# Layer-0 expert gate and up projections with their output index on partitions, from a static copy of the tile's weights

## The reference, cut to what matters

```
x = hidden_states.reshape(-1, 256)
probs = softmax(x @ w_router)
top_vals, top_idx = top_k(probs, 2)
for e in range(8):
    w_e = sum(where(top_idx == e, top_vals, 0))
    g = x @ w_gate[e] * 0.5          # 256 -> 512
    u = x @ w_up[e]                  # 256 -> 512
    h = silu(g) * u @ w_down[e] * 0.25
    out += w_e[:, None] * h
```

## Time and profile before

| what | us |
|---|---|
| median of 3 runs | 1102.59 |
| lowest, highest | 1101.93, 1104.66 |
| profiled execution, own time | 1102.88 |
| profiled execution, span | 1101.0 |
| graph attention of layer 0 | 10 to 186 |
| routing, similarity | 186 to 206 |
| mixture of layer 0, 23 tiles | 206 to 345 |
| reload, second layer's attention and mixture | 345 to 1101 |

### The profile page before, as it was taken

One profiled execution on the slowest core, in us unless ns is written; L12 is line 12 of the kernel. 1 busy time (PEld: TensorE's weight loads), 2 busy tenths in 40 slices (PEclk: granted clock), 3 DMA queues, 4 the chain that ended last, 5 costly groups with the idle time before them and its releaser, 6 DMA issues.

```text
span 1101.0 us, 20158 instructions
## 1 busy us (share of the span) xinstructions
PE 1006.5 (91%) x5934; PEld 821.6 (75%) x5934; DVE 868.8 (79%) x2642; ACT 613.7 (56%) x1748; POOL 430.9 (39%) x372
## 2 busy tenths in 40 slices
PE   4788877999996489999999999999998999999997
PEld 2455545466663368999999999999887888888886
DVE  6999996577773889878777877777868888788877
ACT  4789983533232377777787777777952222222231
POOL 5798892633321233323332333222422232233231
PEclk9968887699998699999999999999999999999999
DMA  9700003011113111010101000000011111111111
GB/s 286 257 1 2 1 2 110 27 47 49 44 39 117 60 39 49 1 39 2 49 1 40 13 23 1 2 1 1 15 30 29 44 43 52 48 43 44 56 43 38
DMA packets 49459, 49.25 MB, mean 45 GB/s; under 512 B 4896, under 2 KB 42464, under 8 KB 49376
## 3 DMA queue, kind: packets, MB, share of 16 engines
q1 hardware_dynamic: 45888, 40.83, 11.8%
q0 software_dynamic: 2208, 6.03, 1.8%
q10 hardware_dynamic: 1280, 1.38, 0.5%
HBM read 43.11 MB, written 5.11 MB: 44 GB/s over the span
## 4 chain that ended last, share of the span: by engine, by line
PE 71%; DVE 12%; ACT 7%; POOL 5%; issue 4%; DMA 1%; SPq 0%; DVEq 0%; ACTq 0%; POOLq 0%
PE bank L57 13%; PE bank L58 13%; PE bank L59 13%; PE bank L957 6%; PE bank L978 4%; PE bank L852 4%; PE bank L860 4%; PE bank L879 4%; PE bank L967 3%; PE bank L979 2%; POOL rest L1418 2%; POOL alpha L1421 1%; DVE alpha L1626 1%; ACT alpha L1069 1%; ACT alpha L1054 1%
## 5 line engine op out<-in xcount | busy, mean ns | idle before, releaser
L1483 POOL TENSOR_TENSOR rot_s<-swap,rq 128x512 f32<-128x512 f32 x64 | 88.5, 1384 | 194.7 <-ACT swap L1261 194.6
L1137 ACT ACTIVATE silu<-bank 128x512 f32<-128x512 f32 x66 | 39.4, 598 | 173.6 <-PE bank L59 173.6
L2066 DVE TENSOR_TENSOR o_ring<-bank,o_ring 128x256 fp32r<-128x256 f32 x128 | 54.2, 424 | 80.2 <-ACT o_ring L1290 78.7
L1274 ACT ACTIVATE prob<-prob,pmin 128x128 f32<-128x128 f32 (+1 forms) x256 | 113.3, 447 | 5.4 <-DVE pmin L2047 5.4
L957 PE MATMUL bank<-kv,norm 128*128 128x128 f32 (+1 forms) x512 | 106.1, 330 | 6.1 <-DVE norm L2040 5.9
L1889 DVE SCALAR_TENSOR_TENSOR xs<-bank,wt,xs 128x256 f32<-128x256 f32 x264 | 109.0, 476 | 0.1
L1439 POOL TENSOR_TENSOR gate_r<-gate_w,gate_r 128x256 fp32r<-128x256 f32 x31 | 36.4, 1175 | 177.3 <-ACT gate_r L1130 177.3
L1290 ACT ACTIVATE o_ring<-bank 128x256 fp32r<-128x256 f32 x128 | 48.3, 378 | 76.4 <-PE bank L979 76.3
L57 PE MATMUL bank<-wo_r,o_ring 128*128 128x256 f32 x256 | 82.5, 322 | 0.0
L1867 DVE TENSOR_TENSOR hidf<-silu,bank 128x512 f32<-128x512 f32 x66 | 45.4, 688 | 44.9 <-ACT silu L1137 43.2
L2059 DVE TENSOR_SCALAR prob<-prob,pinv 128x128 f32<-128x128 f32 (+1 forms) x256 | 76.9, 343 | 4.6
(11 more groups left out here) (304 smaller groups left out, 3087.0 us busy)
## 6 DMA issues: line engine op xcount, KB each, us to landing
gate_w<-in_Wg SPq DMA_DIRECT2D x33, 128.0 KB, 2.1
up_w<-in_Wu SPq DMA_DIRECT2D x33, 128.0 KB, 2.3
down_w<-in_Wd SPq DMA_DIRECT2D x33, 128.0 KB, 2.3
w_all<-in_w_gate SPq DMA_DIRECT2D x8, 512.0 KB, 10.5
w_all<-in_w_up SPq DMA_DIRECT2D x8, 512.0 KB, 10.3
w_all<-in_w_down SPq DMA_DIRECT2D x8, 512.0 KB, 10.6
wq_g<-in_Wq SPq DMA_DIRECT2D x4, 1024.0 KB, 5.8
wo_g<-in_Wo SPq DMA_DIRECT2D x4, 1024.0 KB, 5.5
```

Source lines behind the costliest of these rows:

```text
L1274: ins = act.activation(prob[:, u % 4, nt * P:nt * P + (nt + 1) * P], prob[:, u % 4, nt * P:nt * P + (nt + 1) * P], ACT.Exp, bias=pmin[:, u ...
L1483: pool.tensor_tensor(rot_s[:, m % 2].rearrange("p (b n) -> p b n", b=2), swap[:, m % 2].rearrange("p (b n) -> p b n", b=2), bcast(tab[:, 1 ...
```

## The change

Gate and up get their operands the other way round: a 128x128 block of expert weights is the stationary operand and the 128 turned token rows move, in four blocks of the inner index. The result has the inner index on partitions, which is what `down` wants. `turn_hidden` and `copy_hidden` go; VectorE's product is written to `hgT` (now a tile of its own in the place of `hid`), and waits for `y_ready` in place of `hid_turned`.

The stationary operand is read at a static address, from `tile_w`, two buffers of 2048 elements a partition that lie in `norm` and `actT`. VectorE fills both for tiles 0 and 1 at the end of the routing. For the tiles from 2 on, ScalarE copies gate and up of the tile's expert with two instructions (`copy_weights`), after the copy of the turned rows; it waits until up of two tiles before has been computed, and TensorE's gate waits for it (`w_copied`).

```diff
 def gate(j):                                                    # TensorE
     ats[j] = pe.value_load(w_at[0:1, j:j + 1], min_val=0, max_val=(E0 - 1) * WROW)
     pe.wait_ge(S["xgT_copied"], j + 1)
     if j >= 2:
         pe.wait_ge(S["gact_done"], j - 1)
-    for c in range(HC):
-        mm = pe.matmul(GB[j % 2][:], xgT[:, j % 2, c, :], flat_w[:, bass.ds(ats[j] + c * I0, I0)],
-                       start=c == 0, stop=c == HC - 1)
+    if j < 2:
+        pe.wait_ge(S["w_first"], j + 1)
+    else:
+        pe.wait_ge(S["w_copied"], j - 1)
+    for i in range(I0 // P):
+        for c in range(HC):
+            mm = pe.matmul(GB[j % 2][:, i * P:i * P + P], tile_w[j % 2][:, c * I0 + i * P:c * I0 + i * P + P],
+                           xgT[:, j % 2, c, :], start=i == 0 and c == 0, stop=i == I0 // P - 1 and c == HC - 1)
...
-def turn_hidden(j):
-    pe.wait_ge(S["hid_done"], j + 1)
-    if j >= 1:
-        pe.wait_ge(S["hgT_copied"], j)
-    else:
+def down(j):
+    pe.wait_ge(S["hid_done"], j + 1)
+    if j == 0:
         pe.wait_ge(S["sim_copied"], T)
-    for c in range(I0 // P):
-        mm = pe.transpose(HB[:, c * P:c * P + P], hid[:, j % 2, c * P:c * P + P], ident[:])
...
 for j in range(TILES + 1):
     if j < TILES:
         gate(j)
-    if j >= 1:
-        turn_hidden(j - 1)
-    if j < TILES:
         up(j)
     if j + 1 < TILES:
         turn_rows(j + 1)
...
-def copy_hidden(j):                                             # ScalarE
-    act.wait_ge(S["hid_turned"], j + 1)
-    if j >= 2:
-        act.wait_ge(S["y_ready"], j - 1)
-    act.activation(hgT[:, j % 2].rearrange("p c n -> p (c n)"), HB[:], ACT.Copy).then_inc(S["hgT_copied"], 1)
+def copy_weights(j):
+    at = act.value_load(w_at[0:1, j:j + 1], min_val=0, max_val=(E0 - 1) * WROW)
+    act.wait_ge(S["up_ready"], j - 1)
+    for m in range(2):
+        ins = act.activation(tile_w[j % 2][:, m * GU:m * GU + GU], flat_w[:, bass.ds(at + m * GU, GU)],
+                             ACT.Copy)
+    ins.then_inc(S["w_copied"], 1)
...
 for j in range(TILES + 1):
     if j < TILES:
         gates(j)
-    if j >= 1:
-        copy_hidden(j - 1)
     if j + 1 < TILES:
         copy_rows(j + 1)
+    if 2 <= j + 1 < TILES:
+        copy_weights(j + 1)
     if j >= 1:
         copy_out(j - 1)
...
+dve.wait_ge(S["w_all_in"], 16 * 3 * E0)                         # VectorE, end of router0
+dve.wait_ge(S["rows_out"], 16 * B)
+for j in range(2):
+    at = dve.value_load(w_at[0:1, j:j + 1], min_val=0, max_val=(E0 - 1) * WROW)
+    dve.tensor_copy(tile_w[j][:, 0:2 * GU], flat_w[:, bass.ds(at, 2 * GU)]).then_inc(S["w_first"], 1)
...
 if j >= 2:                                                      # VectorE, the product
-    dve.wait_ge(S["hid_turned"], j - 1)
-dve.tensor_tensor(hid[:, j % 2, :], gact[:, j % 2, :], UB[j % 2][:], ALU.mult).then_inc(S["hid_done"], 1)
+    dve.wait_ge(S["y_ready"], j - 1)
+dve.tensor_tensor(hgT[:, j % 2].rearrange("p c n -> p (c n)"), gact[:, j % 2, :], UB[j % 2][:], ALU.mult
+                  ).then_inc(S["hid_done"], 1)
```

More of the change, by code:

```diff
@@ L162, in build @@
         wa_tmp1 = flat(kv)[:, 2 * D:6 * D].rearrange("p (a n) -> p a n", a=4)
-        hgT = flat(norm)[:, 0:2 * I0].rearrange("p (a c n) -> p a c n", a=2, c=I0 // P)
+        tile_w = (flat(norm), flat(actT))
         x1T = route[:].rearrange("p a t e -> p (a t e)")[:, 0:2 * HC * N].rearrange("p (a c n) -> p a c n", a=2, c=HC)
@@ L219, in build @@
         gact = sb_sparse("gact", [P, 2, I0])
-        hid = sb_sparse("hid", [P, 2, I0])
+        hgT = sb_sparse("hgT", [P, 2, I0 // P, P])
         yg = sb_sparse("yg", [P, 3, D])
@@ L315, in build @@
             "xg_turned", "xgT_copied", "gate_ready", "up_ready", "gact_done", "hid_done",
-            "hid_turned", "hgT_copied", "y_ready", "y_copied", "tok_added", "sig_kept", "sig_scaled", "gam_half",
+            "w_first", "w_copied", "y_ready", "y_copied", "tok_added", "sig_kept", "sig_scaled", "gam_half",
             "qk_ready", "qk_copied", "sim_ready", "sim_copied", "sig_done", "gam_done",
@@ L833, in sparse_mixture @@
             def sparse_mixture():
-                GB, UB, XB, HB, YB = bank[0:2], bank[2:4], bank[4], bank[5], bank[6:8]
+                GB, UB, XB, YB = bank[0:2], bank[2:4], bank[4], bank[6:8]
                 flat_w = w_all[:].rearrange("p e m n -> p (e m n)")
@@ L858, in up @@
                         pe.wait_ge(S["hid_done"], j - 1)
-                    for c in range(HC):
-                        mm = pe.matmul(UB[j % 2][:], xgT[:, j % 2, c, :], flat_w[:, bass.ds(ats[j] + (GU + c * I0), I0)],
-                                       start=c == 0, stop=c == HC - 1)
+                    for i in range(I0 // P):
+                        for c in range(HC):
+                            mm = pe.matmul(UB[j % 2][:, i * P:i * P + P],
+                                           tile_w[j % 2][:, GU + c * I0 + i * P:GU + c * I0 + i * P + P],
+                                           xgT[:, j % 2, c, :], start=i == 0 and c == 0, stop=i == I0 // P - 1 and c == HC - 1)
                     mm.then_inc(S["up_ready"], 1)
-                def turn_hidden(j):
+                def down(j):
                     pe.wait_ge(S["hid_done"], j + 1)
-                    if j >= 1:
-                        pe.wait_ge(S["hgT_copied"], j)
-                    else:
+                    if j == 0:
                         pe.wait_ge(S["sim_copied"], T)
-                    for c in range(I0 // P):
-                        mm = pe.transpose(HB[:, c * P:c * P + P], hid[:, j % 2, c * P:c * P + P], ident[:])
-                    mm.then_inc(S["hid_turned"], 1)
-                def down(j):
-                    pe.wait_ge(S["hgT_copied"], j + 1)
                     if j >= 2:
@@ L1180, in sparse_mixture @@
             def sparse_mixture():
-                GB, XB, HB, YB = bank[0:2], bank[4], bank[5], bank[6:8]
+                GB, XB, YB = bank[0:2], bank[4], bank[6:8]
+                flat_w = w_all[:].rearrange("p e m n -> p (e m n)")
                 def copy_rows(j):
@@ L1794, in router0 @@
                     chain.link(dve.tensor_reduce(w_tok[:, k, :], pick[:], X, ALU.add))
+                flat_w = w_all[:].rearrange("p e m n -> p (e m n)")
+                dve.wait_ge(S["w_all_in"], 16 * 3 * E0)
[3 more added lines that the diff above has]
+                    dve.tensor_copy(tile_w[j][:, 0:2 * GU], flat_w[:, bass.ds(at, 2 * GU)]).then_inc(S["w_first"], 1)
             def router1(half, part):
```

## The result

The changed kernel takes 1123.71 us (median of 4 runs, 1122.96 to 1124.80); the kernel before took 1103.62 in the same comparison. The ratio is 1.0181, with a 95% interval of 1.0167 to 1.0195: slower, by 20.1 us. The forecast was 1123.5. The profiled execution has a span of 1123.0 us, 22.0 more than before.

The account below looks back on a forecast made before the run. TensorE alone bound the mixture at 5.83 us a tile; with the change a loop through ScalarE's copies would. +22.4 us in the loop and -1.5 at the end gave +20.9, 1123.5 us, range 1111 to 1134.

Parts of the forecast that it names:

- Gate and up at 1.78: Layer 0 mixture, TensorE: gate and up cost 1.78 us each instead of 1.72, +0.12 us a tile.
- rival C: Gate and up on TensorE: weight loads lie bare, 3.0 us each, 1178 us in all; chance 0.03.
- Turning goes: Mixture, TensorE: the hidden values' four transposes, 0.44 us a tile, leave the chain; -1.5 us from gate 22 on.
- The copies: ScalarE, from tile 2 on: two weight copies of 128x1024 a tile, 1.04 us each, 1.98 together.
- The register load: ScalarE, behind the row copy's wait: the first weight copy starts 0.70 us after the row copy starts.
- The loop: Mixture, gate to gate through ScalarE's copies: 6.90 us a tile, 144.9 against 122.49 us, +22.4.
- The first two tiles: VectorE after the last w_tok: two 128x2048 weight copies of 2.56 us each, costing the total 0.
- Rival B: Mixture stage: the clock falls as TensorE stands 16% of the time, 21 periods take 168 us, 1147 us; chance 0.10.
- Rival D: Between row copy and gate: weight copies keep ahead of TensorE, 5.51 us a tile, 1094 us; chance 0.06.

Follow-up runs that it names:

- the first experiment: Against the changed kernel, ScalarE copies the next tile's weights before the next tile's rows; 1096.25 us, ratio 0.9929 to the kernel before.

## Why the prediction was right

*Gate and up at 1.78.* Measured 1.79 for up and, after a wait, 2.02 for the gate, against 1.78 and 2.04. The value projection in the earlier trace rows was the right row: the shape and the fresh blocks were the same. The rule of the Trainium skill weighed there ("TensorE: Matmul & The Clock Gate", section "Back-to-back issue gap") would have had an estimated 0.8 us more a tile; the measured price of the operand order is 2.5 to 3.8 us in all, so for these fp32 matmuls the measurement stands against it, and against rival C.

*Turning goes.* The forecast had 0.44 us a tile, and a net 1.5 at the end. The end came out at 7.28 us from gate 22 to the end of the last down, the sum to the hundredth, and the kernel before without the turning shows 12.1 us for the whole of it.

*The copies.* Mean 1.05 us each and 2.01 for two, against 1.04 and 1.98. The Trainium skill, in "ScalarE: Activation LUTs", section "What ACT_TABLE_LOAD costs", has 186 ns + 0.833 ns an element and an overlap of about 93 ns; an estimate from it is 1.04 and 1.99, and the trace agrees.

*The register load.* 0.64 us from row copy to first weight copy against 0.70. Moving the load alone gave 0.36 us a tile. On VectorE the same load was put too low: from the last w_tok's end (203.80) to the first copy (204.85) it is 1.05 us and not 0.6, without consequence here.

*The loop.* 6.86 us a tile (215.17 to 359.31 for 21 tiles) against 6.90: 144.1 in place of 144.9. Its place in the queue is shown from two sides: the copies moved, or left out, give the same 1096; half of them taken out of the gate's wait gives back 20.4 us of an expected 20.

*The first two tiles.* VectorE's copies took 1.33 and 1.21 us, half of my 2.56; the first gate waited for the row copy and not for them.

*Rival B* did not come about: the clock in the stage stayed at 1.00. Its price was also summed wrongly. By its own terms, 4.04 us doubled for 38% of the time add 1.5 us a tile, so the 21 periods take 177 us and not 168, and the kernel some 1156 and not 1147.

*Rival D* is what the first experiment turns the kernel into: 5.52 us a tile for 5.51, 1096.25 us for 1094. The prediction had it as a matter of price ("between row copy and gate"), while its real way in was the order of two calls.

That the total came out within 0.2 us is in part luck. The forecast added 20.9 us to the 1102.59 of the first three runs; the kernel before took 1103.62 in the comparison, 1.0 more, and the change cost 20.1, 0.8 less, since the loop was 0.8 us under my sum. In the spans there is another such shift: everything in this profiled execution is already 1.4 us late when the routing ends, before any changed instruction: the last w_tok starts at 203.58 against 202.19. Such a shift differs from one run to the next (the first gate starts between 205.9 and 208.8 in the runs above), so the comparison of medians, 20.1 us, is nearer to the stage's own 20.1 (21.65 more in the loop, 1.52 less at the end) than the span's 22.0.

## What to carry to other kernels

An engine that is idle half the time can still set the pace: ask behind which wait a new piece of work is queued, and when the engine that needs it will ask for it. Here 2 us of copies a tile cost 28 us behind a wait (1123.71 against 1095.68 without them), and ahead of that wait nothing that can be measured, which turned a loss of 1.8% into a gain of 0.7%. A register load took about 0.6 us of its engine's queue here, and more on VectorE, so issue it right behind an instruction that runs at least as long, with no wait between the two. When a wait is shown for a whole block of data, check whether its reader needs only the first half to start: here that alone gave back 20 us.

## What was not expected of the hardware

The granted clock stayed at 1.00 with TensorE standing 1.10 us of 6.86 in each tile, with 1.29 of 7.05, and with 1.65 of 7.41. It fell for a while behind single waits of 1.89 and 1.96, and was 0.87 with 2.39 to 2.41 in tiles that take 8.15 at full clock. There the fall cost nearly as much as the added wait itself. No run here has steady waits between 1.65 and 2.39, so where the fall sets in is open.

VectorE's copy of 128x2048 fp32 within SBUF took 1.21 to 1.33 us where ScalarE takes 2.01 for two halves. While the first two of VectorE's copies ran, one gather instruction on POOL took 2.00 us, where the kernel before has 0.95 for it:

```profile
204.85 1.33 DVE L1799 COPY norm<-w_all 128x2048 f32 x1 [1.05 <-issue]
...
205.44 2.00 POOL L1490 DMA_INDIRECT xg<-x_rows,row_id  x1 [0.30 <-issue]
```

It is the same in the run with VectorE's register load behind its copy: gathers that ran beside no copy took 0.96 to 0.97 us, and one that started at 310.03, within a copy of 309.75 to 310.97, took 1.78. That the two engines hinder each other is what these rows suggest; no run was made to show by what.
